# Part of a mixture-of-experts kernel: where VectorE makes one low part and two table pieces, and how many rows TensorE's first step of an expert works on

## What is computed

```python
def reference(x, L0_tok_codebook, L0_tok_W1, ..., L0_ffn_Wg):
    ...
    h = _L0_tok_ref(x, L0_tok_codebook, L0_tok_W1, L0_tok_b1, L0_tok_W2, L0_tok_b2)
    h = h + _L0_attn_ref(_layernorm(h, axis=-1), L0_attn_Wz, L0_attn_bz, L0_attn_Wh, L0_attn_bh)
    h = h + _L0_ffn_ref(_layernorm(h, axis=-1), L0_ffn_w1s, L0_ffn_w2s, L0_ffn_w3s, L0_ffn_W1, L0_ffn_W2, L0_ffn_W3, L0_ffn_Wg)
    return h

def geglu(x, w1, w2, w3):
    return jax.nn.gelu(x @ w1, approximate=False) * (x @ w2) @ w3
    ...
    shared = geglu(xf, w1s, w2s, w3s)
    idx = jnp.argmax(xf @ Wg, axis=-1)
    for e in range(N_EXPERTS):
        y = geglu(xf, W1[e], W2[e], W3[e])
        final = final + jnp.where((idx == e)[:, None], y, 0.0)
```

## Time and profile before

| what | us |
|---|---|
| median of 3 runs | 483.22 (482.52 to 484.07) |
| the profiled execution | 483.58 |
| its span in the trace | 481.9 |
| TensorE busy (matmuls) | 474.4, 98% |
| TensorE weight loads | 424.9, 88% |
| VectorE busy | 330.8, 69% |
| ScalarE busy | 246.9, 51% |
| GpSimd busy | 77.6, 16% |

### The profile page before, as it was taken

How to read it: one execution, slowest core, us unless ns; L and a number is a source line. 1 busy time by engine, 2 the same in 40 slices (tenths; PEclk the granted TensorE clock), 3 DMA queues, 4 the chain that set the end, 5 groups by cost and what they waited for, 6 DMA issues and landing times.

```text
span 481.9 us, 8608 instructions
## 1 busy us (share of the span) xinstructions
PE 474.4 (98%) x3052; PEld 424.9 (88%) x3053; DVE 330.8 (69%) x559; ACT 246.9 (51%) x376; POOL 77.6 (16%) x92
## 2 busy tenths in 40 slices
PE   8999999999999999999999899999999999999997
PEld 7999888889888888888789899889999998999887
DVE  3658678578776887768654678537876696678464
ACT  3767774575664464443434457336545463645321
POOL 4431031011010010102450002100101011011460
PEclk9999999999999999999999999999999999999999
DMA  5952121001220002200434467504553465341292
GB/s 167 340 162 86 37 76 56 33 23 44 61 73 1 1 0 78 100 0 23 153 122 100 135 209 248 182 24 173 181 203 122 183 238 207 120 141 72 58 333 90
DMA packets 26425, 56.07 MB, mean 116 GB/s; under 512 B 7248, under 2 KB 19664, under 8 KB 22416
## 3 DMA queue, kind: packets, MB, share of 16 engines
q1 hardware_dynamic: 19312, 43.45, 26.7%
q0 software_dynamic: 2976, 8.14, 5.0%
q10 hardware_dynamic: 4096, 3.93, 2.9%
HBM read 43.16 MB, written 12.35 MB: 115 GB/s over the span
## 4 chain that ended last, share of the span: by engine, by line
PE 89%; DVE 7%; ACT 2%; issue 1%; another core or an unknown queue 1%; ACTq 0%; DVEq 0%
PE ps L285 24%; PE ps L286 23%; PE ps L287 23%; PE ps L816 6%; PE ps L818 3%; PE ps L514 2%; PE ps L846 2%; DVE hT L1256 1%; DVE ps L1262 1%; PE ps L848 1%; PE ps L622 1%; PE ps L657 1%; PE ps L669 1%; PE ps L704 1%; DVE w_slots L1284 1%
## 5 line engine op out<-in xcount | busy, mean ns | idle before, releaser
L285 PE MATMUL ps<-xW,w_slots 128*128 128x256 f32 (+1 forms) x256 | 72.5, 283 | 1.3 <-DVE hW L1618 1.3
L286 PE MATMUL ps<-xW,w_slots 128*128 128x256 f32 (+1 forms) x256 | 71.6, 280 | 0.0
L287 PE MATMUL ps<-xW,w_slots 128*128 128x256 f32 (+1 forms) x256 | 71.6, 280 | 0.0
L1256 DVE TENSOR_TENSOR hT<-ps,hT 128x512 fp32r<-128x512 f32 x64 | 44.0, 687 | 35.7 <-ACT hT L984 16.2
L491 POOL DMA_INDIRECT y_tokens<-y_rows,to_rows x30 | 31.4, 1048 | 183.2 <-DVE y_rows L1659 173.5
L285 PEld LDWEIGHTS ps<-xW,w_slots 128*128 128x128 f32 x256 | 48.8, 191 | 2.1 <-issue 1.5
L286 PEld LDWEIGHTS ps<-xW,w_slots 128*128 128x128 f32 x256 | 48.9, 191 | 0.0
L287 PEld LDWEIGHTS ps<-xW,w_slots 128*128 128x128 f32 x256 | 48.9, 191 | 0.0
L816 PE MATMUL ps<-w_slots,hW 128*128 128x512 f32 x128 | 46.7, 401 | 0.0
L995 ACT ACTIVATE hT<-ps 128x512 fp32r<-128x512 f32 x32 | 19.1, 598 | 53.6 <-DVE ps L1262 50.5
L1133 ACT ACTIVATE w_slots<-stage 128x2048 fp32r<-128x2048 f32 x24 | 45.8, 1909 | 0.0
(11 more groups left out here) (213 smaller groups left out, 1284.5 us busy)
## 6 DMA issues: line engine op xcount, KB each, us to landing
stage<-ew_in SPq DMA_DIRECT2D x24, 1024.0 KB, 4.8
x_sorted<-zero_row SPq DMA_DIRECT2D x32, 128.5 KB
stage<-w1s_in SPq DMA_DIRECT2D x2, 1024.0 KB, 8.3
fetched<-y_tokens SPq DMA_DIRECT2D x4, 512.0 KB
x_pair<-x_sorted ACTq DMA_DIRECT2D x7, 256.0 KB, 2.8
x_one<-x_sorted ACTq DMA_DIRECT2D x7, 256.0 KB
out_rows<-fetched SPq DMA_DIRECT2D x3, 512.0 KB
first_stage<-tok_w_in SPq DMA_DIRECT2D x1, 1024.0 KB, 5.2
```

The source lines that it names most:

```text
L285: pe.matmul(dst, lhs_hi, rhs_hi, start=start, stop=False, skip_group_check=shares_bank)
L286: pe.matmul(dst, lhs_hi, rhs_lo, start=False, stop=False, skip_group_check=shares_bank)
L287: return pe.matmul(dst, lhs_lo, rhs_hi, start=False, stop=stop, skip_group_check=shares_bank)
L1256: dve.tensor_tensor(hT[:, c % RING, 1, :], ps[:, bank, :], f32(hT[:, c % RING, 0, :]), ALU.subtract).then_inc(h_lo, 1)
```

## The change

Three edits. (1) In expert 0 VectorE makes `single_rows_lo(0)` and `split_piece_lo(23)` behind `window_lo(0)` and no longer ahead of it. (2) `place_singles` moves from chunk 47 to chunk 51. (3) Step 0 of experts 1 to 7 also branches on `more`; so TensorE's sequencer reads `more` ahead of that step. In the opening expert `more` is read earlier too, but its step 0 stays at 256 rows.

```diff
@@ tensor engine, expert() @@
                 pe.wait_ge(pair_lo, e + 1)
                 if not opening:
                     one_transposes(m)
+                more = more_of(pe, e)
                 pe.wait_ge(split_lo, e * 3 + 5)
...
                 else:
-                    window_up(e, 0, odd)
+                    window_up_of(more, e, 0, odd)
                     window_down(e * PAIRS, PAIRS - 1, not odd)
                     count = singles_of(pe, e)
-                more = more_of(pe, e)
                 with pe.If(count > 0):
@@ vector engine, chunks @@
-                if c == RANK + 3:
+                if c == RANK + 7:
+
                     place_singles()
@@ vector engine, expert() @@
                 window_gated(e, 0)
                 if opening:
-                    single_rows_lo(0)
-                    for n in SPLIT_PIECES[ROW]:
-                        split_piece_lo(n)
+
                     spread_unread()
                 else:
                     take_tile(s + e * 2 - 1, 4)
                 window_lo(e, 0)
-                if not opening:
+                if opening:
+                    single_rows_lo(0)
+                    for n in SPLIT_PIECES[ROW]:
+                        split_piece_lo(n)
+                else:
                     take_tile(s + e * 2, 5)
```

## The result

The kernel after takes **501.39 us** (median of 6 runs, 498.01 to 503.58), the kernel before 483.25 beside it (6 runs): ratio 1.0368, 95% interval 1.0351 to 1.0385. The change costs 18 us where 481.9 was forecast. The profiled execution took 500.41, its span is 498.6.

A forecast was written before the change was run, and what follows sets the result against it. The prediction took TensorE to bound the kernel (89% of the chain that ended last). Gains of 0.7 (edit 1), 0.6 (edit 3) and 0 (edit 2) sum to 1.3, from a median of 483.22 to 481.9; range 480.7 to 483.3.

The forecast's parts named there:

- the loop outgrows the instruction store: Rival: expert loop's TensorE code no longer fits, two jumps back wait 1.6 us each, 3.2 slower, 485.1; chance 0.10.
- further blocks: Expert loop: upper bound of 8 us lost if more instruction blocks than those at the jumps back miss too.
- Edit 1: Expert 0: stop before step 2 goes, 1.50 us gained there; worth 0.7 us (0.4 to 1.2) from expert 1 on.
- 1.22 at step 3: Expert 0, step 3: a new stop of 0.28 us for `window_lo(1)` leaves 1.22 of the 1.50 gained.
- 0.5 lost again before expert 1: Before expert 1's step 0: TensorE's sequencer, with added register load and branch, comes late and loses 0.5 of 1.22 us.
- 0.3 for the sequencer coming sooner: Before expert 1: TensorE's emptier queue lets eight matmuls in faster, some 0.3 us, an estimate with bounds 0 and 0.4.
- all is gained: Rival: the sequencer does not delay expert 1, so 1.2 + 0.6 = 1.8 us gained, 481.4; chance 0.13.
- what is late next?: Question asked in expert 0 after the stop before step 2 goes; answered with a 0.28 us stop before step 3.
- Edit 3's rows: Three experts' first steps on 192 rows, not 256: 3 x 0.20 = 0.6 us gained (bounds 0 and 0.65).
- Edit 2: `place_singles` moved to chunk 51: cost nothing, up to 0.15 us; gain taken as 0, bound 1.1.
- The stop of 1.1 us in chunk 50: Router, TensorE waiting for VectorE's `add_rows`: expected to stay; rival that it goes too, 1.1 us more, 480.8, chance 0.12.
- The sum: Whole kernel: 0.7 + 0.6 + 0 = 1.3 us gained, giving 481.9.

The follow-up runs named there:

- after_slot160: The kernel after, unchanged in instructions, with TensorE's expert loop beginning at place 160 of a 256-instruction block: 499.31 us, ratio 1.0352.
- before_slot208: The kernel before, unchanged in instructions, with its expert loop beginning at place 208 of a 256-instruction block: 482.21 us, ratio 0.9999.
- after_slot100: The kernel after, unchanged in instructions, with TensorE's expert loop beginning at place 100 of a 256-instruction block: 483.01 us, ratio 1.0014.
- light loads: The kernel after with weight loads of experts 2 to 7 cut from 1 MB to 128 KB, the instruction list unchanged: 491.61 us, ratio 1.0187.
- edit1_slot0: The kernel before with edit 1 alone, TensorE's expert loop placed at the start of a 256-instruction block: 481.36 us, ratio 0.9976.
- after_slot0: The kernel after with all three edits, TensorE's expert loop placed at the start of a 256-instruction block: 480.77 us, ratio 0.9967.
- edits12: The kernel after without edit 3, so edits 1 and 2 alone, no place stated for the loop: 482.23 us, ratio 0.9995.
- after_hint: The kernel after with a hint at the expert loop's head that names the jump back: 487.04 us, ratio 1.0102.
- unrun_half: The kernel before with 52 never-run instructions in one of the expert loop's two experts: 500.70 us, ratio 1.0376.

## Why the prediction was wrong

**The step that failed: the rival "the loop outgrows the instruction store".** It named the mechanism, the view and the stretch (q8 rows between 326 and 426), and it came true. Three things in it were wrong.

*Its chance, 0.10.* I set it by an increase of 6% and had no row that shows how much code is kept. But the loop doesn't lie at a block's start, and by the account above it is held in whole blocks and needs the one behind its end not to be asked for. At an unlucky place (208 in after, 160 in after_slot160) 1,730 instructions touch 8 blocks and, by that account, ask for a ninth. "No row shows the store near its end" was a count of rows that couldn't show it: the q8 rows of before_slot208 and after_slot100, at the edge, look like those of a loop with room, and the step is sharp (52 instructions that never run cost 18 us).

*Its price, 3.2.* I gave a missed jump 1.6 us: 1.2 for the packet, 0.7 to ask for it, and nothing for the time from the packet to the branch's end or for a load ahead of it. The nearest to the 0.7 in the trace of before are six branches of 0.33 to 0.43 us (at 268.3, 287.4, 292.1, 318.9, 324.3 and 430.6), with a q8 packet 0.66 to 0.78 behind the end of each; with light loads the packet started 1.0 and 0.95 behind the start of the two jumps. It takes 3.5 to 3.8 with light loads, and 6.3 and 5.1 behind a weight load. The bound of 8 for "further blocks" took blocks as missing one by one. The runs show a packet for each of them in every round: nine in the second and nine in the third, some of them waited for at forward branches (L892 took 2.0 and 1.9 us in these rounds). And the clock's fall (to 0.64 and 0.79 behind the first, 1.7 us) adds to the stops.

*Its weight in the range.* It was left outside on that chance; at its own price of 3.2 it would have said 485.1, still 16 us short.

**Edit 1 was right, and its limit was not.** The forecast had 1.22 at step 3 (a new stop of 0.28 there; the trace of edit1_slot0 has one of 0.17) and 0.5 lost again before expert 1. Measured against before_slot208, which has neither the edit nor the stop of chunk 50: from step 1's first matmul to step 3's, edit1_slot0 takes 275.62 - 268.04 = 7.58 us where before_slot208 takes 277.05 - 268.27 = 8.78, so 1.20. To expert 1's first matmul it is 281.36 - 268.04 = 13.32 for 282.69 - 268.27 = 14.42, so 1.10. The 0.5 for the sequencer is 0.1; with edit 3's load and branch in it (after_slot0: 281.78 - 268.51 = 13.27) it is no more. The forecast had 0.3 for the sequencer coming sooner, a guess without a row; the measured figure is 0.8. From `window_lo(2)`'s end to the register load at L307 it is 279.51 - 278.65 = 0.86 us in before_slot208 and 278.44 - 278.37 = 0.07 in edit1_slot0. That an emptier queue does it is the forecast's reading. The rival "all is gained" was right there. VectorE's rows in edits12, against the earlier trace rows:

```profile
269.23 0.18 DVE L1666 SCALAR_TENSOR_TENSOR unread<-row_ids,unread_by 128x30 f32<-128x30 f32 x1
269.45 0.19 DVE L1669 TENSOR_TENSOR to_rows<-row_ids,unread 128x30 int32<-128x30 f32 x1
269.99 0.69 DVE L1619 TENSOR_TENSOR hW<-ps,hW 128x512 fp32r<-128x512 f32 x1 [0.35 <-ACT hW L1124]
270.60 0.41 DVE L1398 TENSOR_TENSOR xTp<-ps,xTp 128x256 fp32r<-128x256 f32 x1
```

`spread_unread` fits beside ScalarE's high part and VectorE even waits 0.35 for it, as the working said.

**At the old place that gain doesn't last.** edits12 lost it again within expert 1, in two branches, 1.6 us at L892 and 2.3 at L803 (from 290.5), with a q8 packet at 284.2 and at 290.3, each within 0.2 us of the end of a 1 MB load. The first and TensorE's stops in edits12:

```profile
L892 PEldq COMPARE_BRANCH  x1: 1599/1599/1599, 285.0 to 285.0; - x1
```

```profile
286.75 0.38 PE L285 MATMUL ps<-xW,w_slots 128*128 128x256 f32 x1 [0.57 <-issue]
...
293.66 0.54 PE L704 MATMUL ps<-ident,x_pair 128*128 128x128 f32 x3 [0.90 <-issue]
```

This is the question "what is late next?", which I asked of engines and not of the instruction queue. In the loop's first round the code is still being loaded between the weight loads (six q8 packets from 282 to 326 in edits12), so TensorE coming 1.3 us earlier only waits there. At a block's start the fetches fall otherwise (at 285.7 and 291.4 in edit1_slot0, where L892 took 0.35), and 1.2 is left.

**Edit 3's rows.** 120 matmuls on 192 rows at L285, as forecast; 3 x 0.20 = 0.6 against a measured 0.9 (0.4 to 1.3 by its interval). Load and branch ahead of six first steps show no stop. The interval holds the 0.6 that came from the rows, 8 ns for 64 rows less.

**Edit 2** at 0 was right. The stop of 1.1 us in chunk 50, for which I kept 1.1 as a bound and 0.12 as a chance, isn't a property of the kernel before: it is missing from the profile of before_slot208, which has edit 2 no more than before has, and stands with 0.5 in that of after, which has it.

**The sum.** 1.3 was forecast for the three edits, and where the loop has room they bring 1.6 (1.1 to 2.1). The 1.3 lies in that interval, with edit 1 forecast too low (0.7 for 1.2) and edit 3 perhaps too (0.6 for 0.9). So the working was near in what it summed, and wrong by 18 us about what it had left to a chance.

## What to carry to other kernels

Before a loop body grows, count its instructions in blocks of 256 (252 to a packet by the count here) from where it lies, and see how far it reaches into the eighth. In these runs loops that ended at place 38 to 42 of the eighth block kept their jump back fast, and those that ended at 92 or further lost 16 to 18 us; 1,730 instructions at a block's start fitted with seven blocks (larger loops weren't tried). Code that never runs counts in full (52 such instructions cost the whole 18 us). If a small edit to a sequencer's code costs tens of us, look at the instruction queue between two jumps back first, and put the loop elsewhere before you take the edit back. In code that still streams in, a long forward branch can be a wait for a DMA (1.6 to 3.7 us at L892 here), often behind the large load that is running, so a gain just ahead of it can vanish there.

## What the runs showed of the hardware

- The jump back took 0.21 to 0.22 us where no q8 packet came with it (before, after_slot0, after_slot100); branches that ended only behind their packet took 3.6 us on quiet DMA queues (after_hint), 3.5 and 3.8 beside loads of 128 KB, and behind a 1 MB load 5.1 to 7.0 (the 7.0 in unrun_half).
- A q8 packet brought 16.4 KB, for 252 records of TensorE in the unrolled part. It took 1.1 us on average (0.6% of 16 engines x 498.6 us over 45 packets in after). At both jumps back of after the block came when the 1 MB load had ended or was within 0.3 us of it; at place 160 it came 1.0 and 0.5 us before the load's end.
- With the same loop of 1,730 instructions the kernel took 480.8 with its head at place 0 of a block, 483.0 at 100, 499.3 at 160 and 501.4 where it had come to lie.
- After a stop of 3.9 us TensorE's granted clock was 0.64 and 0.79 in the next two stretches of 3 us, then 1.00.
- With a hint at the loop's head (after_hint) the jumps took 0.23 and 0.22 us where they took 6.3 and 5.1, and the q8 rows of two rounds were gone.
